# Identity products on TensorE at the start of two attention phases, an earlier load of the key bias, and a new order in cross-attention's first batch

## The chip, the core and the metric

The program runs on one core of a Trainium2 chip. The time is device microseconds from the start of the program to its end. A core has five engines with queues of their own: PE (TensorE, matrix products; its weight loads are a row of their own, PEld), DVE (VectorE), ACT (ScalarE), POOL (GpSimd) and SP (SyncE, which here issues all bulk DMAs). They meet only at semaphores, and each queue is worked off in program order. TensorE's clock has two levels in this trace, 1.2 and 2.4 GHz; the profile prints the granted clock as a share of the higher one, 0.50 or 1.00.

## What is computed

A post-norm decoder layer in float32: 16 batches of 100 tokens, width 512. Self-attention has 16 heads of 32, cross-attention 16 query heads and 4 key/value heads of 128 over a context of 361 tokens, and the last third is a mixture of 8 experts.

```python
x = _layernorm(x + _L0_attn_ref(x, w_q, w_k, w_v, w_o))
x = _layernorm(x + _L0_xattn_ref(x, ctx, mask, Wq, bq, Wk, bk, Wv, bv, Wo, qn_w, kn_w))
x = _layernorm(x + _L0_ffn_ref(x, ...))
...
# cross-attention
k = (encoder_hidden_states @ Wk + bk)   # 16 x 361 x 4 x 128
v = (encoder_hidden_states @ Wv + bv)
q, k = _rmsnorm(q, qn_w), _rmsnorm(k, kn_w)
probs = softmax(q k^T * scale + mask)
out = (probs v) @ Wo
```

## The kernel before

The program is a chain of blocks: self-attention over the batches, cross-attention over the batches, the experts. Between two blocks all engines meet at a barrier. Inside a block each engine has its own program, written out by hand in the order in which it is to be worked off, and `pe.wait_ge(sem, n)` makes the engine stand until another one has signalled. There is no scheduler: an instruction that waits holds back everything behind it on its engine.

Precision: the big products are done as three products of split operands. `product3` (L59 to L72; the product itself is L70) takes a high and a low part of each side and issues high by high, high by low and low by high. So each raw weight matrix is first split, the high part by ACT (`split_hi`) and the low part by DVE (`split_lo`), and TensorE waits for that (`w_lo`). Plain float32 products are used for the projections of q and k in self-attention (L258), the scores (L305), probabilities by values (L355) and all transposes (a product with the identity, `ident_s`).

Self-attention, first batch (`i == 0`). PE does the projections, the scores (L305), then waits for the split of w_v, does the value product on bank 7, transposes four groups of probabilities (L343) as POOL finishes each, multiplies them by the values (L355), projects the next pair's keys (L258), and does the output product on `a_woh`. From batch 1 on the queries of cross-attention (`a_Wqh`) are computed between those steps. After the last batch (`i == B`) three key products of cross-attention's first batch (`context_keys`) are laid between the last query work; the first of them waits for the context's low part (`head.ctx_lo`) and then for the split of Wk (`head.w_lo`, 2).

Cross-attention, before its loop. A batch's 361 context tokens are three chunks c of 121. Of each chunk there are keys (bias added, squared and summed on DVE in `key_squares`, the root on POOL, scaled on DVE in `key_norm`, transposed on PE in `transpose_keys`, split by ACT and DVE in `keys_hi` and `keys_lo`) and values (`values`, `values_hi`, `values_lo`). The bias bk is loaded by the first DMA of the block. DVE starts with `key_squares(0, 0)`, which needs it. PE does `values(0, c)` and `transpose_keys(0, c)` in turn for c = 0, 1, 2.

Cross-attention's loop. A batch j has four steps s, one for each key/value head, with four query heads h in each. PE interleaves the scores of step s, the transposes of the probabilities of the step before (`transpose_probs`, L855), parts of the keys of batch j + 1 and parts of the output product; `values_product` (probabilities by values of the step before) ends the step. In step 2 the order is: one quarter of the output product, `transpose_keys(j + 1, 0)`, the 12 products of `keys(j + 1, 2)`, and then `values_product`. Batch 0 has less work to interleave, since there is no batch before, and besides it ACT and DVE split the eight pieces of Wo, two at the end of each step.

## Time and profile before

| | us |
|---|---|
| median of 3 runs | 1596.74 |
| the runs | 1594.62 to 1597.72 |
| the profiled execution's own time | 1593.47 |
| its span | 1591.6 |
| PE busy | 1474.6 (93%) |
| DVE busy | 949.7 (60%) |
| mean granted clock of TensorE | 0.968 |

In rows of a timeline, the columns are the start in us, the duration in us (for a row that merges several instructions, from the start of the first to the end of the last), engine, source line, operation, tiles out<-in, partitions and shapes, and the count. In brackets stands the idle time of the engine right before it, and who ended it. Float32 products are recorded as two instructions each (x32 for 16 products). In rows of a table by windows, the columns are the stretch, its length, the busy time of each engine with instruction counts, the granted clock, the share of the DMA engines and GB/s.

### The profile page before, as it was taken

To read this page: it belongs to the slowest core of one execution; us is meant where nothing else is said; L and a number is where in the kernel's file an instruction comes from. 1 tells how busy PE (TensorE), PEld (TensorE's weight loads), DVE (VectorE), ACT (ScalarE), POOL (GpSimd) and SP (SyncE) were. 2 spreads that over 40 slices of the span, in tenths; PEclk is the share of its full clock that TensorE was granted. 3 is DMA by queue.
4 is the path that set the end of the run, shared out by engine and by line. 5 is a ranking of instruction groups with operands and counts; after the bars stand their busy time and mean duration, and the time that the engine had idled before them with its cause. 6 is when DMAs were issued, how large, how long until landed. Compare 5 with 4: busy or idle time off the path is not lost. (4 is left out here: it accounts for less than half of the span.)

```text
span 1591.6 us, 27704 instructions
## 1 busy us (share of the span) xinstructions
PE 1474.6 (93%) x8462; PEld 1206.2 (76%) x8462; DVE 949.7 (60%) x3585; ACT 662.4 (42%) x1789; POOL 648.4 (41%) x1000
## 2 busy tenths in 40 slices
PE   6999999999988689999999999999999999489967
PEld 6777877877866478888888888888888887367744
DVE  3666666666666565566655665566555665653457
ACT  4434334334343253444444444444444445343346
POOL 1324324324334364444444444344444443373164
PEclk8999999999999989999999999999999999789988
DMA  6221121121132332121111112111121213375373
GB/s 208 93 85 63 72 91 64 72 86 69 67 117 89 122 112 71 56 59 58 43 60 55 62 36 69 56 59 55 42 61 55 64 37 117 142 207 174 125 235 102
DMA packets 60669, 139.62 MB, mean 88 GB/s; under 512 B 10150, under 2 KB 20746, under 8 KB 59588
## 3 DMA queue, kind: packets, MB, share of 16 engines
q1 hardware_dynamic: 56008, 123.72, 23.5%
q0 software_dynamic: 4576, 14.95, 3.3%
q8 instruction: 31, 0.51, 0.1%
q14 instruction: 54, 0.44, 0.1%
HBM read 94.18 MB, written 44.46 MB: 87 GB/s over the span
## 5 line engine op out<-in xcount | busy, mean ns | idle before, releaser
L1253 POOL TENSOR_TENSOR b_pcarry<-b_half 128x1 f32<-128x1 f32 x173 | 47.6, 275 | 392.1 <-DVE b_rinv L1123 354.4
L1014 ACT ACTIVATE b_probs<-b_probs,b_nmax 100x361 f32<-100x361 f32 x256 | 152.1, 594 | 79.5 <-DVE b_nmax L1117 79.1
L70 PE MATMUL bank<-b_kTh,b_q 128*100 128x362 f32 x512 | 172.4, 337 | 9.3 <-DVE b_kTl L1099 6.0
L1117 DVE CUSTOM_DVE_ANT_0 b_probs<-bank,b_mask 100x361 f32<-100x361 f32 x256 | 135.3, 529 | 52.9 <-issue 45.2
L1278 POOL TENSOR_SCALAR b_probs<-b_probs,b_rinv 100x361 f32<-100x361 f32 x256 | 163.6, 651 | 0.0
L1110 DVE TENSOR_TENSOR b_pTl<-bank,b_pTh 121x400 fp32r<-121x400 f32 x192 | 109.7, 572 | 53.1 <-ACT b_pTh L1009 53.0
L1052 ACT ACTIVATE b_oTh<-bank,b_bv 128x400 fp32r<-128x400 f32 x64 | 38.1, 595 | 233.1 <-PE bank L70 233.1
L1009 ACT ACTIVATE b_pTh<-bank 121x400 fp32r<-121x400 f32 x192 | 96.6, 504 | 85.6 <-PE bank L855 81.3
L855 PE MATMUL bank<-ident,b_probs 100*121 100x100 f32 x768 | 111.3, 268 | 6.4 <-POOL b_probs L1278 5.6
L855 PEld LDWEIGHTS bank<-ident,b_probs 100*121 100x121 f32 x768 | 108.6, 188 | 9.0 <-POOL b_probs L1278 7.1
L70 PE MATMUL bank<-b_Woh,b_oTh 128*100 128x512 f32 x256 | 111.1, 434 | 1.4 <-DVE b_oTl L1181 1.4
L70 PEld LDWEIGHTS bank<-b_kTh,b_q 128*100 128x100 f32 x512 | 85.3, 167 | 29.3 <-issue 14.0
L70 PE MATMUL bank<-a_Wqh,a_x1Th 128*100 128x512 f32 x256 | 100.7, 393 | 2.7 <-DVE a_qn L547 1.5
L70 PE MATMUL bank<-a_Wqh,a_x1Tl 128*100 128x512 f32 x256 | 101.0, 394 | 0.0
L70 PE MATMUL bank<-b_Woh,b_oTl 128*100 128x512 f32 x256 | 100.9, 394 | 0.0
L70 PE MATMUL bank<-b_Wol,b_oTh 128*100 128x512 f32 x256 | 100.9, 394 | 0.0
L70 PE MATMUL bank<-a_Wql,a_x1Th 128*100 128x512 f32 x256 | 100.6, 393 | 0.0
L1181 DVE SCALAR_TENSOR_TENSOR b_oTl<-bank,b_bv,b_oTh 128x400 fp32r<-128x400 f32 x64 | 40.5, 633 | 97.6 <-ACT b_oTh L1052 97.6
L424 ACT ACTIVATE a_probs<-a_probs,a_nmax 100x100 f32<-100x100 f32 x256 | 92.8, 367 | 4.4 <-DVE a_nmax L500 4.4
L627 POOL TENSOR_TENSOR a_probs<-a_probs,a_rinv 100x400 f32<-100x400 f32 x64 | 54.7, 855 | 93.4 <-DVE a_rinv L507 93.3
L70 PE MATMUL bank<-b_Wkh,b_ctxh 128*121 128x512 f32 x192 | 82.2, 428 | 11.3 <-DVE b_kn L1080 8.2
L70 PE MATMUL bank<-b_kTl,b_q 128*100 128x362 f32 x256 | 84.3, 329 | 0.0
(259 smaller groups left out, 3949.4 us busy)
## 6 DMA issues: line engine op xcount, KB each, us to landing
b_q<-q_d SPq DMA_DIRECT2D x64, 400.0 KB, 3.1
q_d<-a_qo SPq DMA_DIRECT2D x62, 400.0 KB, 2.4
b_ctxr<-in_ctxT SPq DMA_DIRECT2D x48, 242.0 KB, 3.9
y_d<-c_y SPq DMA_DIRECT2D x32, 256.0 KB
c_Eraw<-in_expert_w SPq DMA_DIRECT2D x10, 512.0 KB, 7.0
a_stage<-in_Wq SPq DMA_DIRECT2D x4, 1024.0 KB
stage<-in_Wo SPq DMA_DIRECT2D x8, 512.0 KB, 4.4
a_xTr<-in_xT SPq DMA_DIRECT2D x8, 400.0 KB
```

The source lines that it names most:

```text
L70: mm = eng.matmul(out, lhsT=l(c), rhs=r(c), start=first and k == 0, stop=last and k == n - 1)
L424: e = act.activation(probs[:, r, c, :], probs[:, r, c, :], ACT.Exp, scale=-1.0, bias=nmax[:, h:h + 1], accum_out=psums[:, r, c:c + 1])
L627: pool.tensor_tensor(probs[:, r], probs[:, r], rinv[:, r].unsqueeze(2).to_broadcast([S, DC, S]), ALU.mult).then_inc(pn_rdy, 1)
L855: mm = pe.transpose(t_bank[c % 2][0:KT, h * S:(h + 1) * S], probs[:, s % 2, h, c * KT:(c + 1) * KT], ident_s[0:S, 0:S])
L1009: act.activation(pTh[:, c, :], t_bank[c % 2][0:KT, 0:XG * S], ACT.Copy).then_inc(pt_hi, 1)
L1014: act.activation(p, p, ACT.Exp, scale=-1.0, bias=nmax[:, s % 2, h:h + 1], accum_out=psums[:, s % 2, h:h + 1]).then_inc(e_rdy, 1)
L1052: act.activation(oTh[:, kv, :], o_bank[:, 0:XG * S], ACT.Identity, bias=bv_s[:, kv:kv + 1]).then_inc(o_hi, 1)
L1110: dve.tensor_tensor(pTl[:, c, :], t_bank[c % 2][0:KT, 0:XG * S], pTh[:, c, :].bitcast(F32), ALU.subtract).then_inc(pt_lo, 1)
L1117: dve.tensor_tensor_reduce(out=probs[:, s % 2, h, 0:SE], in0=s_bank[h % 2][0:S, 0:SE], in1=mask_s[:], scale=-1.0, scalar=BIG, op0=ALU.add, ...
L1181: dve.scalar_tensor_tensor(out=oTl[:, kv, :], in0=o_bank[:, 0:XG * S], scalar=bv_s[:, kv:kv + 1], in1=oTh[:, kv, :].bitcast(F32), op0=ALU.add,
L1253: pool.tensor_tensor(pcarry[:, k:k + 1], half_s[:, 0:1], half_s[:, 0:1], ALU.add)
L1278: pool.tensor_scalar(p, p, rinv[:, s % 2, h:h + 1], 1.0, ALU.mult, ALU.mult).then_inc(p_rdy, 1)
```

## The change

There are three parts.

1. `keep_busy(pe, out, ident, count)` issues `count` float32 products of the 128 x 128 identity with itself into a bank that is free at that place; nobody reads the result. It stands at seven places on PE: 8 before the wait for the split of w_v in self-attention's batch 0; 8, 4, 4 and 4 before the waits for the four groups of probabilities there; 12 between the two waits of `context_keys(0)`; 16 in cross-attention's batch 0 behind the first score of step 1, ahead of the first `transpose_probs`; 7 ahead of `transpose_keys(1, 1)`. That makes 63 products.
2. The load of bk is moved from the first DMA of cross-attention's block to SP's queue in batch `B - 2` of self-attention, into a tile that lives outside both blocks.
3. Cross-attention's first batch has another order: ahead of the loop on PE, ACT and DVE, and in step 2 of batch 0 on PE, where `values_product` now stands ahead of `keys(1, 2)`.

```diff
+def keep_busy(pe, out, ident, count):
+    for _ in range(count):
+        pe.matmul(out, lhsT=ident[:], rhs=ident[:], start=True, stop=True)
...
@@ self-attention, sync
                     for n in range(2):
                         sp.dma_start(head.pieces[n][1], head.pieces[n][0]).then_inc(head.w_raw[n], 16)
                         sp.dma_start(head.ctxr[:, n], ctxT[n]).then_inc(head.ctx_in[n], 16)
+                    sp.dma_start(head.bk_s[:], bk.partition_broadcast(KT)).then_inc(head.bk_in, 16)
@@ self-attention, tensor
                 pe.wait_ge(head.ctx_lo, c + 1)
+                if c == 0:
+                    keep_busy(pe, first_key_bank(bank, c)[:, 0:P], ident_s, 12)
                 pe.wait_ge(head.w_lo, 2)
...
                     if is_int and i == 0:
+                        keep_busy(pe, bank[6][:, 0:P], ident_s, 8)
                         pe.wait_ge(w_lo, 1)
...
                     for r in range(SR):
+                        if is_int and i == 0:
+                            keep_busy(pe, bank[6][:, 0:P], ident_s, 4 if r else 8)
                         pe.wait_ge(pn_rdy, 4 * i + r + 1)
@@ cross-attention, sync
-            sp.dma_start(bk_s[:], bk.partition_broadcast(KT)).then_inc(bk_in, 16)
             load_q(0, 0, 0)
@@ cross-attention, tensor
             def transpose_keys(jn, c):
-                pe.wait_ge(k_rdy, 3 * jn + c + 1)
                 if c == 1:
                     pe.wait_ge(kt_lo, 3 * jn + 1)
+                    if isinstance(jn, int) and jn == 1:
+                        keep_busy(pe, kv_bank[KEY_T_BANK[c]][:, 0:P], ident_s, 7)
+                pe.wait_ge(k_rdy, 3 * jn + c + 1)
...
-            for c in range(KC):
-                values(0, c)
-                transpose_keys(0, c)
+            values(0, 0)
+            values(0, 1)
+            transpose_keys(0, 0)
+            values(0, 2)
+            transpose_keys(0, 1)
+            transpose_keys(0, 2)
...
                         if now:
                             scores(j, s, h, par)
+                        if first and s == 1 and h == 0:
+                            keep_busy(pe, kv_bank[0][:, 0:P], ident_s, 16)
                         if before:
                             transpose_probs(n - 1, (s + 3) % 4, h)
...
                         if not last:
                             transpose_keys(j + 1, 0)
+                            if first:
+                                values_product(n - 1, s - 1, j)
                             keys(j + 1, 2)
...
-                    if before:
+                    if before and not (first and s == 2):
                         values_product(n - 1, (s + 3) % 4, j)
@@ cross-attention, vector, ahead of the loop
             key_squares(0, 1)
             key_norm(0, 0)
             values_lo(0, 0)
+            key_norm(0, 1)
+            key_squares(0, 2)
             keys_lo(0, 0, 0)
-            key_squares(0, 2)
-            key_norm(0, 1)
             values_lo(0, 1)
-            keys_lo(0, 1, 0)
             key_norm(0, 2)
             values_lo(0, 2)
+            keys_lo(0, 1, 0)
             keys_lo(0, 2, 0)
```

ACT's order ahead of the loop follows PE's: both value copies of chunks 0 and 1, then `keys_hi(0, 0)`, the value copy of chunk 2, then the other two `keys_hi`.

On DVE, ahead of cross-attention's loop, these rows stood behind the squares of chunk 1 before (`b_kn<-b_kn,b_krs` is `key_norm`, `b_Vl` is `values_lo`, `b_kTl` is `keys_lo`, `b_kn<-bank,b_bk` opens `key_squares` of chunk 2):

```order
L1093 TENSOR_TENSOR b_kn<-b_kn,b_krs 121x512
L1105 TENSOR_TENSOR b_Vl<-bank,b_Vh 121x512
L1099 TENSOR_TENSOR b_kTl<-bank,b_kTh 128x4x121
L1080 TENSOR_TENSOR b_kn<-bank,b_bk 121x512
...
L1093 TENSOR_TENSOR b_kn<-b_kn,b_krs 121x512
L1105 TENSOR_TENSOR b_Vl<-bank,b_Vh 121x512
L1099 TENSOR_TENSOR b_kTl<-bank,b_kTh 128x4x121
L1093 TENSOR_TENSOR b_kn<-b_kn,b_krs 121x512
L1105 TENSOR_TENSOR b_Vl<-bank,b_Vh 121x512
L1099 TENSOR_TENSOR b_kTl<-bank,b_kTh 128x4x121
```

and now, with the bias tile named bk:

```order
L1116 TENSOR_TENSOR b_kn<-b_kn,b_krs 121x512
L1128 TENSOR_TENSOR b_Vl<-bank,b_Vh 121x512
L1116 TENSOR_TENSOR b_kn<-b_kn,b_krs 121x512
L1103 TENSOR_TENSOR b_kn<-bank,bk 121x512
...
L1122 TENSOR_TENSOR b_kTl<-bank,b_kTh 128x4x121
L1128 TENSOR_TENSOR b_Vl<-bank,b_Vh 121x512
L1116 TENSOR_TENSOR b_kn<-b_kn,b_krs 121x512
L1128 TENSOR_TENSOR b_Vl<-bank,b_Vh 121x512
L1122 TENSOR_TENSOR b_kTl<-bank,b_kTh 128x4x121 x2
```

`key_norm` of chunk 1 has moved ahead of the squares of chunk 2, and the three `keys_lo` have moved behind the norms that TensorE's next transposes wait for.

On PE, step 2 of cross-attention's batch 0, the end of the step stood like this before (`b_kn` is `transpose_keys(1, 0)`, `b_Wkh` the keys of chunk 2, `b_pTh` is `values_product`, `b_kTh` the next step's score):

```order
L893 MATMUL bank<-ident,b_kn 128x121 x4
L70 MATMUL bank<-b_Wkh,b_ctxh 121x512
L70 MATMUL bank<-b_Wkl,b_ctxh 121x512
L70 MATMUL bank<-b_Wkh,b_ctxl 121x512
...
L70 MATMUL bank<-b_pTh,b_Vh 128x400
L70 MATMUL bank<-b_pTl,b_Vh 128x400
L70 MATMUL bank<-b_pTh,b_Vl 128x400
...
L70 MATMUL bank<-b_kTh,b_q 100x362
```

and now:

```order
L906 MATMUL bank<-ident,b_kn 128x121 x4
L70 MATMUL bank<-b_pTh,b_Vh 128x400
L70 MATMUL bank<-b_pTl,b_Vh 128x400
L70 MATMUL bank<-b_pTh,b_Vl 128x400
...
L70 MATMUL bank<-b_Wkh,b_ctxh 121x512
L70 MATMUL bank<-b_Wkl,b_ctxh 121x512
L70 MATMUL bank<-b_Wkh,b_ctxl 121x512
...
L70 MATMUL bank<-b_kTh,b_q 100x362
```

The nine products of `values_product` have changed places with the twelve of the keys.

## Rows read from the trace of the kernel before

**Rows 1.** The page, busy time of each engine.
```profile
PE 1474.6 (93%) x8462; PEld 1206.2 (76%) x8462; DVE 949.7 (60%) x3585; ACT 662.4 (42%) x1789; POOL 648.4 (41%) x1000
```

**Rows 2.** Table by windows, one stretch near each phase's start.
```profile
26.00:27.00 1.00, 1.00 (x3) 0.59 (x3) 1.00 (x1) 0.00 (x0) 0.00 (x0) 0.50 0.64 98
...
600.00:605.00 5.00, 5.00 (x24) 4.21 (x23) 1.92 (x9) 1.83 (x5) 0.00 (x0) 0.72 0.56 201
```

**Rows 3.** PE's timeline, self-attention's first batch, and one step of the second.
```profile
14.69 5.58 PE L258 MATMUL bank<-a_xTr,a_wq 128*128 128x200 f32 x32
...
25.07 0.45 PE L70 MATMUL bank<-a_wvh,a_xTh 128*100 128x512 f32 x1 [1.94 <-DVE a_wvl L463]
...
34.99 0.91 PE L343 MATMUL bank<-ident,a_probs 100*100 100x100 f32 x4 [0.54 <-POOL a_probs L627]
35.82 3.56 PE L355 MATMUL bank<-a_pT,a_v 100*32 100x100 f32 x32
39.31 7.48 PE L258 MATMUL bank<-a_xTr,a_wk 128*128 128x200 f32 x32
46.49 0.53 PE L70 MATMUL bank<-a_woh,a_oTh 128*100 128x512 f32 x1
...
49.16 0.39 PE L70 MATMUL bank<-a_woh,a_oTl 128*100 128x512 f32 x1
...
70.64 1.99 PE L355 MATMUL bank<-a_pT,a_v 100*32 100x100 f32 x32
```

**Rows 4.** PE's timeline, the first key product behind self-attention's last batch.
```profile
503.58 0.57 PE L70 MATMUL bank<-b_Wkh,b_ctxh 128*121 128x512 f32 x1 [3.10 <-DVE b_Wkl L468]
...
506.50 0.63 PE L70 MATMUL bank<-b_Wkl,b_ctxh 128*121 128x512 f32 x1
```

**Rows 5.** DVE's timeline, cross-attention ahead of its loop.
```profile
532.11 0.07 DVE L1128 MEMSET b_probs<- 100x16 f32 x1
536.33 0.69 DVE L1080 TENSOR_TENSOR b_kn<-bank,b_bk 121x512 f32<-121x512 f32 x1 [4.14 <-DMA b_bk<-in_bk]
...
539.59 0.68 DVE L1093 TENSOR_TENSOR b_kn<-b_kn,b_krs 121x512 f32<-121x512 f32 x1
```

**Rows 6.** POOL's timeline, the root of the second chunk's sums.
```profile
540.41 1.01 POOL L1269 TENSOR_TENSOR b_krs<-b_krs,b_half 121x4 f32<-121x4 f32 x1
```

**Rows 7.** PE's timeline, cross-attention ahead of its loop and the first score.
```profile
532.14 0.46 PE L70 MATMUL bank<-b_Wvh,b_ctxh 128*121 128x512 f32 x1 [2.10 <-PEq L105]
...
540.33 1.07 PE L893 MATMUL bank<-ident,b_kn 121*128 121x121 f32 x4 [5.15 <-DVE b_kn L1093]
...
551.05 0.38 PE L70 MATMUL bank<-b_kTh,b_q 128*100 128x362 f32 x1 [1.65 <-DVE b_kTl L1099]
```

**Rows 8.** PE's timeline, batch 0, from step 1 to the first transposes of step 2.
```profile
559.13 1.13 PE L855 MATMUL bank<-ident,b_probs 100*121 100x100 f32 x4 [4.41 <-POOL b_probs L1278]
...
564.33 0.63 PE L70 MATMUL bank<-b_Wkh,b_ctxh 128*121 128x512 f32 x1
...
570.00 0.67 PE L855 MATMUL bank<-ident,b_probs 100*121 100x100 f32 x4
```

**Rows 9.** DVE's timeline, batch 0: masked scores, first and last of step 2, first of step 3.
```profile
571.75 0.53 DVE L1117 CUSTOM_DVE_ANT_0 b_probs<-bank,b_mask 100x361 f32<-100x361 f32 x1
...
575.15 0.53 DVE L1117 CUSTOM_DVE_ANT_0 b_probs<-bank,b_mask 100x361 f32<-100x361 f32 x1
...
588.77 0.53 DVE L1117 CUSTOM_DVE_ANT_0 b_probs<-bank,b_mask 100x361 f32<-100x361 f32 x1
```

**Rows 10.** PE's timeline, batch 0, end of step 2 to end of step 3.
```profile
576.41 0.63 PE L893 MATMUL bank<-ident,b_kn 121*128 121x121 f32 x4
580.50 0.76 PE L70 MATMUL bank<-b_Wkh,b_ctxh 128*121 128x512 f32 x1 [3.46 <-DVE b_kn L1080]
...
585.74 0.35 PE L70 MATMUL bank<-b_pTh,b_Vh 121*128 121x400 f32 x1
...
598.12 0.63 PE L893 MATMUL bank<-ident,b_kn 121*128 121x121 f32 x4 [1.88 <-DVE b_kn L1093]
```

More of the change, by code:

```diff
@@ L96, in first_key_bank, with self_attention_phase @@
     return bank[(0, 1, 7)[c]]
-def self_attention_phase(nc, sem, head, ctxT, x_nat, xT, w_q, w_k, w_v, w_o, Wq, bq, qn_w, kn_w, causal, ident, ident_s, x1_d, q_d):
+def self_attention_phase(nc, sem, head, ctxT, bk, x_nat, xT, w_q, w_k, w_v, w_o, Wq, bq, qn_w, kn_w, causal, ident, ident_s, x1_d, q_d):
     with ExitStack() as ctx:
@@ L676, in cross_attention_phase @@
         mask_s = sb("b_mask", [S, SE])
-        bk_s = sb("b_bk", [KT, XKV * XHD])
+        bk_s = head.bk_s
         bv_s = sb("b_bv", [P, XKV])
@@ L1026, in expert_hi @@
                 act.activation(first_pieces[n][2], first_pieces[n][1], ACT.Copy).then_inc(e_hi, 1)
-            for c in range(KC):
-                values_hi(0, c)
-                keys_hi(0, c, 0)
+            values_hi(0, 0)
+            values_hi(0, 1)
+            keys_hi(0, 0, 0)
+            values_hi(0, 2)
+            keys_hi(0, 1, 0)
+            keys_hi(0, 2, 0)
             act.wait_ge(consts, 32)
```

17 lines of the change are left out of this document (9 added, 8 removed).

## The prediction

> **What bounds the kernel.** I read the page first: TensorE is busy for 93% of the span [rows 1], so the loops are bound by it and only places where it stands still or runs at the low clock can give time back. Then the table by windows, for the granted clock: it is 1.00 through nearly all of both loops and 0.50 in a few stretches at the phases' starts [rows 2]. Then PE's timeline there. In self-attention's first batch PE waits 1.94 us for the split of w_v and again before each group of transposes, and what follows runs at 1.2 GHz: the product on `a_pT` takes 3.56 us where the same 16 products in batch 1 take 1.99 [rows 3]. At cross-attention's start PE waits 5.15 us, since DVE waited 4.14 us for the DMA of bk [rows 5, 7]. In batch 0 there are waits of 4.41, 3.46 and 1.88 us [rows 8, 10]. Behind these places PE is nearly always busy, so time gained there should reach the end.
>
> **What an identity product costs.** The trace has none. The nearest row is the projection of q: 16 products, 200 columns wide, in 5.58 us at the high clock, 0.349 each [rows 3]. By columns (128/200) one costs 0.223 us, which I take; 0.349 is the upper bound at this clock, if width does not matter, and twice 0.223, 0.446, is the price at the low clock. The lower bound is nothing beyond the wait it stands in. 63 of them are 14.0 us of work laid into waits; where they outlast the wait, the rest is paid.
>
> A rule of the Trainium skill (TensorE: Matmul & The Clock Gate, LDWEIGHTS) has a weight load take the number of columns over 1.2 ns: 107 ns for 128. With two loads per float32 product, as the x32 for 16 suggests, that gives at least 0.21 us if the streaming is hidden beside it, and some 0.43 if not; by the second figure the groups of four would each outlast their wait.
>
> **Start of self-attention.** The first 8 (1.8 us) fit in the 1.94 us wait, and the clock should not fall. The next 8 stand behind the value product, which ends about 1.7 us earlier at the high clock (12 products at 0.243 instead of about 0.42), and end before the first probabilities. The groups of 4 cost 0.9 us; the waits for POOL are 0.5 to 1.0 us beside transposes at the low clock, which shorten too, so I cost them at nothing; at 0.349 each they would be 0.4 us late three times. The transposes themselves follow ACT and POOL, and do not move. Behind them: the last transposes end 0.4 us earlier, the product on `a_pT` goes from 3.56 to 1.99 (1.57), the projection from 7.18 us (39.31 to 46.49, low clock for its first half) to about 5.7 (the 5.58 of the other one and its tail), 1.5. Sum 3.4 us. The other inputs are there: the split behind the output product is done on DVE at about 41 us, and the new projection ends at 43. Bounds: 0 if the clock falls again, 4 if all of it holds. Low side: minus 2 (below).
>
> **End of self-attention.** PE waits 3.10 us for the split of Wk and then runs at the low clock, from 503.58 to 506.50 seven spacings of 0.417 [rows 4]; at the high clock a product of this width is spaced (49.16 - 46.49)/11 = 0.243 [rows 3]. The 12 identity products (2.7 us) fit in the wait. About eight key products run low, 8 x 0.18 = 1.4 us; behind them waits the transposition of x1, whose input DVE has ready before PE takes it, by its timeline. Gain 1.2 us, bounds -1 (12 x 0.349 = 4.2) and 1.4.
>
> **Cross-attention ahead of the loop.** The load of bk has moved about 90 us earlier, where SP issues it in a third of a microsecond among loads that nothing waits for soon; I cost it at nothing, since PE is fed from loads of the batches before. `load_q(0, 0, 0)` moves up by one issue. DVE then starts at 532.2 instead of 536.33: 4.1 us [rows 5]. From there I follow both queues. The first norm stands 3.26 us behind the start [rows 5]: 535.5, done 536.1. PE does two value groups, 532.14 to 537.8 (24 x 0.24 = 5.7), and the transposes of chunk 0 to 538.2, without the wait of 5.15 us [rows 7]. The norm of chunk 1 follows at 537.3: the second sums are ready at 535.5, and POOL takes 1.8 us with its root of 1.01 [rows 6]. The squares of chunk 2 wait for the transposes and stand at 538.35 to 540.0, the norm of chunk 2 at 542.0, its transposes on PE at 542.7, ACT's copy at 543.3, and the last `keys_lo` at 543.85 to 544.5. The first score starts at 544.6 instead of 551.05 [rows 7]: 6.4 us. Of these 4.1 are the load and 2.3 the order and the clock, which no longer falls. DVE is the last in this chain, not PE. Bounds: 4.1 if only the load counts, 7 if the queues pack tighter.
>
> **Batch 0, step 1.** Behind the first score of step 1, PE waits 4.41 us for POOL [rows 8]. 16 x 0.223 = 3.6 us fit. The stretch 559.13 to 564.33 then lasted 5.2 us at the low clock without a wait; at the high clock PE needs half of it and DVE becomes the bound: in step 2 it needs 3.4 us from the first to the last masked score (571.75 to 575.15) [rows 9]. Gain 5.2 - 3.4 = 1.8 us. The transposes of step 2 at 570.00 follow POOL, which follows the last exponential, so the gain arrives there; bounds 0.5 and 2.6.
>
> **Step 2.** After the transposes at 576.41 PE waits 3.46 us for the bias addition of chunk 1's keys, which DVE reaches behind the splits of Wo [rows 9, 10]. `values_product` does not need it: 9 products of 400 columns, 0.243 x 400/512 x 9 = 1.7 us, now lie in this wait. The keys begin at the same place after the wait, 580.4, and if the clock holds they take 2.8 us instead of 5.24 (580.50 to 585.74): 2.4. Together 4.1 us on PE, of which DVE lets some 3.2 to 4 through: it masks step 3's first score behind the squares of chunk 2, by 585.6 instead of 588.77 [rows 9].
>
> **Step 3.** The wait before the transposes of chunk 2 at 598.12 [rows 10] ends with DVE's norm, which stands 5.3 us behind the last masked score; that moves by the 4 us. The 7 products (1.6 us) stand ahead of it: PE is there at 591.7 on the old scale, done at 593.2, and the norm is due at 594.1. Costed at nothing; 0.9 us is the margin, which at 0.349 each would be just used up. Steps 2 and 3 together: 4.0 us, bounds 1 and 5.5 (the short low-clock stretch behind 600 us could go as well [rows 2]).
>
> **Sum.** 3.4 + 1.2 + 6.4 + 1.8 + 4.0 = 16.8 us. Against the profiled execution, 1593.47, this gives 1576.7; the median of the runs lies 3.3 us above it, and I carry that over: 1596.74 - 16.8 = 1579.9, rounded to 1580. Nothing in the experts' part is touched. Its own low-clock stretches could come out a little different, since all of it starts earlier; I take 2 us either way for that.
>
> **Rivals.**
> A. The clock falls in self-attention's first batch all the same. For it: between the groups of four stand transposes and short waits, and PE fell to 0.50 there with the engine partly busy. Then the groups cost 4 x 0.446 = 1.8 us where about 1.0 is free, 0.8 late three times, the term of 3.4 turns into about -2: 1580 + 5 = 1585.
> A sentence of the Trainium skill (same page, Part 4: PE-mode transpose) speaks for it: transposes do not count as busy for the clock in the way other products do. By it only the identity products would hold the clock there.
> B. DVE and the Wo splits are the bound in batch 0. For it: DVE ends the waits at 551.05, 580.50 and 598.12 [rows 7, 10]. Against it: after the splits it stands idle itself, and the Wo pieces land before ACT asks for them. Then the 1.8 and 4.0 shrink to about 1 in all: 1585.
> C. More than the sum: the fall at 600 us goes as well and DVE's chain packs tighter: 1575.
> D. Slower. The identity products do not hold the clock, and each costs 0.446. Then they outlast their waits: 63 x 0.446 = 28.1 us against some 15.1 us of waits (1.9 + 1.0 + 2.7 + 3.1 + 4.5 + 1.9), 13 us late. Against that stand only the load of bk and the order, 4.1 + 1.7 + 0.5: net 6.6 us slower, 1603. It turns at a cost of (15.1 + 6.3)/63 = 0.34 us each, if no clock is gained. Against it: float32 projections keep the clock at 1.00 while they run.
> E. No change: what starts earlier waits later, at the barrier or in the loop. Against it: in the loops PE's waits are few and short. 1597.
>
> **Chances.** The sum 60%, A 14%, B 10%, C 10%, D 4%, E 2%. The range that holds 8 in 10 is 1574 to 1588: the sum with its bounds, C, and A and B with some of each together. Within 0.2% (3.2 us), about what the measurement can tell from no change: 0.02; slower 0.04; faster 0.94.
>
> **What would show it.** The granted clock at 1.00 from 25 to 50 us, around 504, 538 to 545 and 558 to 565 us. The identity products at 0.22 us each; a wait behind each group of them, not in front of it: if the transposes of probabilities start later than before, the groups are too long. `a_woh` 3.4 us earlier. In cross-attention the bias addition at the memsets, the first score 12.4 us after the start of the block's first product instead of 18.9, the transposes of step 1 8.1 us behind it as before, and from the block's first product to the transposes that stood at 598.12 some 12 us less than the 66.0 of before. The prediction is wrong if these distances hold and the end does not move, or if the clock still reads 0.50 behind an identity group.

## The result and the profile after

The changed kernel takes 1573.61 us (median of 4 runs, 1573.55 to 1574.31), the kernel before in the same comparison 1595.68 (4 runs, 1591.64 to 1597.72): ratio 0.988, 95% interval 0.9863 to 0.9897. That is 22 us less by the medians and 19 by the ratio, where the sum said 16.8. A second comparison on another chip gave 1573.58 against 1590.26 (6 and 11 runs), ratio 0.9898 [0.9877, 0.9918], 16 to 17 us less. The kernel before is the one that wanders: single runs lie between 1586.4 and 1597.7, and its medians in the three comparisons below are 1592.13, 1591.38 and 1590.26 (53 runs), some 5 us under the 1596.74 from which the prediction started.

The page of the changed kernel, busy time and granted clock (PEclk, the span in 40 slices, in tenths of full speed): as many microseconds on TensorE as before [rows 1], 126 instructions more, in a span of 1571.8 us instead of 1591.6.

```profile
span 1571.8 us, 27953 instructions
PE 1474.6 (94%) x8588; PEld 1208.8 (77%) x8588; DVE 949.9 (60%) x3585; ACT 662.0 (42%) x1789; POOL 646.4 (41%) x1000
PEclk9999999999999999999999999999999999689988
```

That the busy time is the same with 63 products more is the first thing to see: what they add, the rest saves by running at 2.4 GHz.

PE's timeline, self-attention's first batch (columns: start, us, engine, line, operation, tiles, count, and the wait before it with what ended it), to set beside [rows 3]:

```profile
22.24 2.05 PE L78 MATMUL bank<-ident 128*128 128x128 f32 x16
24.16 0.47 PE L70 MATMUL bank<-a_wvh,a_xTh 128*100 128x512 f32 x1
...
26.98 1.95 PE L78 MATMUL bank<-ident 128*128 128x128 f32 x16
30.73 0.55 PE L355 MATMUL bank<-ident,a_probs 100*100 100x100 f32 x4 [1.79 <-POOL a_probs L639]
31.11 1.08 PE L78 MATMUL bank<-ident 128*128 128x128 f32 x8
32.17 0.55 PE L355 MATMUL bank<-ident,a_probs 100*100 100x100 f32 x4
...
35.54 2.00 PE L367 MATMUL bank<-a_pT,a_v 100*32 100x100 f32 x32
37.46 5.68 PE L265 MATMUL bank<-a_xTr,a_wk 128*128 128x200 f32 x32
42.84 0.53 PE L70 MATMUL bank<-a_woh,a_oTh 128*100 128x512 f32 x1
```

An identity product costs (24.16 - 22.24)/8 = 0.24 us. The transposes of probabilities still follow each other by 1.44 us, with the groups of four in place of the waits. The product on `a_pT` takes 2.00 us instead of 3.56, and `a_woh` starts 3.65 us earlier, of which 0.82 was there already at the scores, ahead of all identity products (20.09 us after, 20.91 before).

The same view at cross-attention's first keys, at its first score, and in batch 0, to set beside [rows 4, 7, 8, 10]:

```profile
492.59 2.84 PE L78 MATMUL bank<-ident 128*128 128x128 f32 x24
495.94 0.50 PE L70 MATMUL bank<-b_Wkh,b_ctxh 128*121 128x512 f32 x1 [0.51 <-DVE b_Wkl L480]
...
533.65 0.63 PE L906 MATMUL bank<-ident,b_kn 121*128 121x121 f32 x4 [0.75 <-DVE b_kn L1116]
535.73 0.59 PE L70 MATMUL bank<-b_kTh,b_q 128*100 128x362 f32 x1 [1.45 <-DVE b_kTl L1122]
...
540.21 3.73 PE L78 MATMUL bank<-ident 128*128 128x128 f32 x32
544.92 0.67 PE L866 MATMUL bank<-ident,b_probs 100*121 100x100 f32 x4 [0.98 <-POOL b_probs L1301]
...
554.14 0.67 PE L866 MATMUL bank<-ident,b_probs 100*121 100x100 f32 x4 [1.22 <-POOL b_probs L1301]
...
564.65 0.47 PE L70 MATMUL bank<-b_Wkh,b_ctxh 128*121 128x512 f32 x1 [1.81 <-DVE b_kn L1103]
...
567.99 0.57 PE L866 MATMUL bank<-ident,b_probs 100*121 100x100 f32 x4
```

The first score is 15.3 us earlier than in [rows 7]; the wait of 5.15 us has shrunk to 0.75. But the score's product takes 0.59 us where [rows 7] has 0.38: PE had run at the high clock, stood still for 0.75 and 1.45 us, and now the low clock falls on the scores.

DVE's timeline at the same place, to set beside [rows 5]: no wait for `bk`.

```profile
523.42 0.07 DVE L1151 MEMSET b_probs<- 100x16 f32 x1
523.48 0.69 DVE L1103 TENSOR_TENSOR b_kn<-bank,bk 121x512 f32<-121x512 f32 x1
```

The table by windows (columns: window, length, busy time and count of PE, its loads, DVE, ACT and POOL, then the clock):

```profile
26.00:27.00 1.00, 1.00 (x7) 0.70 (x6) 1.00 (x1) 0.00 (x0) 0.00 (x0) 1.00 0.94 392
24.50:42.00 17.50, 15.71 (x127) 14.05 (x126) 9.21 (x44) 12.40 (x41) 3.41 (x4) 1.00 0.42 142
502.00:506.00 4.00, 4.00 (x19) 2.83 (x18) 1.90 (x10) 0.25 (x1) 0.20 (x1) 1.00 0.00 0
523.50:526.90 3.40, 3.40 (x15) 2.69 (x16) 3.22 (x19) 0.38 (x1) 1.21 (x2) 1.00 0.76 185
535.90:539.30 3.40, 3.40 (x12) 2.79 (x12) 1.45 (x8) 1.38 (x4) 0.00 (x0) 0.52 0.00 0
544.00:552.00 8.00, 7.08 (x41) 6.34 (x42) 5.17 (x19) 5.71 (x13) 7.24 (x13) 1.00 0.72 215
564.60:568.00 3.40, 3.35 (x16) 2.77 (x17) 1.25 (x9) 0.00 (x0) 1.49 (x3) 1.00 0.73 272
```

Of these only the stretch of the first scores is near 0.5.

Cut into stretches by starts on PE's timeline (us), the profiled executions compare like this. "Start" is from self-attention's first scores to batch 0's `x1` transposes; "last but one" from batch 13's `x1` transposes to batch 14's; "last" from there to the first product on `Wkh`; "Wk keys" from that to the first product on `Wvh` of cross-attention's block; "to score" from there to the first score; "to step 1" from that to the first transposes of probabilities in step 1; "step 1" and "step 2" from there to those of steps 2 and 3. The rows below the fourth are the experiments of the next section, in their order.

| kernel | start | last but one | last | Wk keys | to score | to step 1 | step 1 | step 2 |
|---|---|---|---|---|---|---|---|---|
| before | 31.93 | 28.69 | 28.21 | 28.56 | 18.91 | 8.08 | 10.87 | 17.87 |
| before, again | 31.28 | 28.82 | 27.70 | 28.56 | 18.84 | 8.08 | 10.87 | 15.47 |
| changed | 29.09 | 26.72 | 26.23 | 27.51 | 12.28 | 9.19 | 9.22 | 13.85 |
| changed, again | 28.95 | 26.70 | 26.61 | 27.52 | 12.27 | 9.21 | 9.21 | 13.84 |
| identity alone | 28.24 | 26.72 | 26.47 | 27.56 | 18.73 | 8.07 | 9.23 | 17.04 |
| load alone | 31.72 | 28.97 | 27.62 | 28.35 | 13.88 | 8.83 | 10.88 | 18.03 |
| load and order | 30.06 | 28.63 | 28.87 | 27.47 | 13.82 | 8.97 | 10.87 | 15.41 |
| identity at start | 28.23 | 26.72 | 27.54 | 28.31 | 18.79 | 8.09 | 10.87 | 17.02 |
| narrow at start | 32.65 | 26.73 | 26.11 | 28.57 | 18.87 | 8.08 | 10.87 | 17.82 |
| no step 1 | 28.28 | 26.71 | 26.99 | 27.05 | 13.83 | 9.15 | 10.87 | 15.40 |
| no groups of 4 | 31.36 | 26.72 | 26.03 | 27.55 | 13.81 | 9.20 | 9.22 | 13.82 |
| old step 2 | 28.21 | 26.69 | 27.85 | 27.52 | 12.28 | 8.97 | 9.22 | 18.24 |
| more places | 28.20 | 26.70 | 27.03 | 27.16 | 13.80 | 8.08 | 9.22 | 13.83 |
| 20 more at start | 31.02 | 26.80 | 27.55 | 27.54 | 12.25 | 8.96 | 9.23 | 13.85 |

From batch 0 to 13 every kernel takes 393.8 to 394.1 us. Before and changed differ by 19.0 us in these stretches and by 0.8 ahead of the first scores, where nothing was edited; what follows step 2 adds 0. The second pair, before again and changed again, differs by 15.3 us in the same stretches (15.2 in the span). Most of the distance between the two pairs lies in step 2, 4.0 against 1.6 us.

The length of "last" goes with the clock in it. In the five kernels whose mean granted clock there is 1.00 it takes 26.0 to 26.6 us; in seven at 0.93 or 0.94, 27.0 to 27.9; in before at 0.92, 28.2; in load and order at 0.84, 28.9.

### The profile page after: what moved, and what is told of

Read it like the earlier page. It is cut to its first block and busy times, and to the rows that moved or that the text cites. A ratio compares the mean times of both kernels' runs of the same rounds, so it can differ in the third digit from the quotient of the medians.

```text
span 1571.8 us, 27953 instructions
## 1 busy us (share of the span) xinstructions
PE 1474.6 (94%) x8588; PEld 1208.8 (77%) x8588; DVE 949.9 (60%) x3585; ACT 662.0 (42%) x1789; POOL 646.4 (41%) x1000
## 5 line engine op out<-in xcount | busy, mean ns | idle before, releaser
L70 PEld LDWEIGHTS bank<-b_kTh,b_q 128*100 128x100 f32 x512 | 85.1, 166 | 28.9 <-issue 13.9
```

The costliest lines, as they stand in the source:

```text
L70: mm = eng.matmul(out, lhsT=l(c), rhs=r(c), start=first and k == 0, stop=last and k == n - 1)
```

## The experiments

**The kernel before, again** (nothing changed): how far does it wander?

> The kernel before, unchanged, run against itself. In the profiled execution of before, one store of queries took 4.8 us to land instead of 2.5, TensorE waited 2.97 us in self-attention's last batch and its clock fell from 473 to 480 us; together some 4 us that the change does not explain. Theory T (an accident of that execution): the ratio is 1.000, single runs lie from 1591 to 1598 as those so far, and the new profile shows no such wait, but perhaps another. Theory U (it belongs to the kernel's schedule): the same wait and the same fall at 473 us are there again.

Ratio 0.9998 [0.9984, 1.0012], 1590.95 us (1586.58 to 1596.04, 12 runs). Its profiled execution has a span 5.7 us shorter than the first one's (1585.9): 1.6 ahead of the first scores, 2.4 in step 2, 0.65 at the start, 0.5 in the last batch. In step 2 both wait 3.46 us ahead of the keys; behind it the clock is 0.50 from 578.9 to 585.7 us in the first execution, and 1.00 through the whole step in the repeat. So in one and the same program the clock falls in one execution and not in another. Theory U was right, though: the wait ahead of batch 14's `x1` transposes is there again, 3.12 us, and the fall of the clock at 473 us behind it.

**The identity products alone**, with load and order as before:

```diff
+                    if is_int and i == 0:
+                        keep_busy(pe, bank[6][:, 0:P], ident_s, 8)
 ...
+                        if first and s == 1 and h == 0:
+                            keep_busy(pe, kv_bank[0][:, 0:P], ident_s, 16)
```

> The 63 identity products at their seven places, with the order and the bk load of before. By the sum of terms: start of self-attention 3.4 to 3.7 us, its end 1.1, step 1 of batch 0 1.7, step 3 0 to 1; the waits of 5.15 and 3.46 us stay and with them the clock's falls behind them. So 6 to 8 us faster than before, ratio about 0.9955. Rival (the identity products also steady the loops, since runs of before differ by 6 us and runs of the changed kernel by 0.8): 10 to 12 us faster, ratio 0.993, and a narrow spread.

Ratio 0.9941 [0.9917, 0.9964], 9.4 us (11.7 by the medians). The start takes 28.24 us, step 1 9.23, the keys 27.56. And a stretch that the prediction had not named is shorter: the last but one, 26.72 us instead of 28.7.

**The load of bk alone:**

```diff
+                    sp.dma_start(head.bk_s[:], bk.partition_broadcast(KT)).then_inc(head.bk_in, 16)
 ...
-            sp.dma_start(bk_s[:], bk.partition_broadcast(KT)).then_inc(bk_in, 16)
```

> Only the load of bk is moved; order as before, no identity products. By the sum: DVE's wait of 4.1 us goes, and the first score comes 4.1 us earlier; ratio 0.9974. Rival (PE or another queue takes the wait's place, for instance the values' high parts on ACT): 0 to 2 us. Second rival (with the shorter wait the clock does not fall any more): up to 6 us.

Ratio 0.9974 [0.9963, 0.9985], 4.1 us. The way to the first score shrinks by 5.0 us (18.9 to 13.88), and the scores behind it lose 0.75 of these to the low clock.

**Load and order without identity products:**

```diff
-            pe.matmul(out, lhsT=ident[:], rhs=ident[:], start=True, stop=True)
```

> The changed kernel with all counts of identity products at zero: the load and the new order alone. By the sum: 4.1 us for the load, 2.3 for the order ahead of the loop, 1.7 for values_product in the wait of step 2 and up to 2.4 if the clock then holds there; 8 to 10 us faster than before, ratio 0.994 to 0.995. Rival (the order is worth nothing without the identity products, because the clock falls anyway): 4 to 5 us, ratio 0.997.

Ratio 0.9956 [0.994, 0.9972], 7.0 us. With the 9.4 of the identity products that makes 16.4 us for the parts, and the whole gave 16.2 (0.0102 of 1590.3) and 19.1 (0.012 of 1595.7): with intervals of 2 to 4 us either way they add up.

The way to the first score, 13.82 us, looks like that of the load alone, 13.88, but the clock differs. With the load alone it is 1.00 all the way; here it is low from 530.4 to 533.8 us, on the values products. Where the clock falls there in kernels with this order the way takes 13.8 us (here, without step 1's products, without the groups of 4, with more places), and where it doesn't, 12.3 (changed, its repeat, old step 2, 20 more at start). The first values products in the kernel without step 1's products, to set beside 523.50:526.90 of the changed kernel in the table above:

```profile
523.80:527.20 3.40, 3.40 (x8) 2.62 (x9) 3.22 (x19) 0.00 (x0) 1.21 (x2) 0.50 0.77 193
```

So at the same clock the new order is worth 1.6 us (13.88 to 12.3).

**Identity products at self-attention's start alone** (28 on the kernel before):

```diff
+                        keep_busy(pe, bank[6][:, 0:P], ident_s, 8)
 ...
+                            keep_busy(pe, bank[6][:, 0:P], ident_s, 4 if r else 8)
```

> The kernel before with the 28 identity products of self-attention's first batch alone. In the kernels without them (before, its repetition, load alone, no identity products) one store of queries at 463 to 470 us lands after 4.8 to 5.1 us, and TensorE waits 2.9 to 3.3 us in the last batch; in the two with them it lands after 2.8 at most and the wait is 1.0. Theory P (place of the program: 56 more instructions in PE's queue shift the point at which PE's next block of instructions is fetched away from these stores): 3.0 to 3.7 us at the start, and 2 to 4 more at 470 us; 1586 us, ratio 0.9965 to 0.9955. Rival T (the stretch at 470 us depended on something else of the change): 3.5 us in all, ratio 0.998.

Ratio 0.9965 [0.9953, 0.9978], 5.6 us. Against the repeat of before, the trace has 3.1 at the start and 2.1 in the last but one batch, 400 us behind the last identity product, where nothing was edited.

**The same 28, eight columns wide:**

```diff
-        pe.matmul(out, lhsT=ident[:], rhs=ident[:], start=True, stop=True)
+        pe.matmul(out[:, 0:8], lhsT=ident[:], rhs=ident[:, 0:8], start=True, stop=True)
```

> As e5, with the 28 products made 8 columns wide instead of 128: as many instructions, little streaming. Theory P: the clock falls at the start as in the kernel before (no gain there), but the store at about 465 us lands in under 3 us and TensorE's wait in the last batch is 1 us: 2 to 4 us faster, ratio 0.998. Rival (it was the earlier time and not the number of instructions): the store takes 4.8 us again, ratio 1.000.

Ratio 0.998 [0.9969, 0.9991], 3.2 us. PE's timeline, and the table by windows behind its first identity products:

```profile
22.50 1.95 PE L78 MATMUL bank<-ident 128*128 128x8 f32 x16
24.43 0.47 PE L70 MATMUL bank<-a_wvh,a_xTh 128*100 128x512 f32 x1
...
33.65 0.89 PE L352 MATMUL bank<-ident,a_probs 100*100 100x100 f32 x4
...
36.76 3.56 PE L364 MATMUL bank<-a_pT,a_v 100*32 100x100 f32 x32
```

```profile
24.50:42.00 17.50, 17.50 (x105) 15.60 (x106) 8.51 (x43) 11.59 (x40) 3.41 (x4) 0.62 0.33 121
```

Eight narrow products take as long as eight wide ones (1.93 and 1.92 us from start to the next product). PE is busy for all of the 17.5 microseconds, with no wait left between the transposes, and its clock falls twice nonetheless, from 25.3 to 28.8 and from 32.2 to 42.4 us: mean 0.62, as in the kernel before (0.64, busy for 13.6 of 17.5). The changed kernel is busy for less, 15.7 us, and holds 1.00. The start is 0.7 to 1.4 us longer than in the kernel before, since at the low clock a group of four takes 1.55 to 1.62 us and delays the transposes behind it. But the last but one batch takes 26.73 us here too. So that gain is not the clock's; it comes with the number of PE's instructions.

**The changed kernel without the 16 of step 1:**

```diff
-                        if first and s == 1 and h == 0:
-                            keep_busy(pe, kv_bank[0][:, 0:P], ident_s, 16)
```

> The changed kernel without the 16 identity products in step 1 of cross-attention's batch 0. By the sum the clock falls in the wait of 4.4 us, and step 1 runs at 1.2 GHz: 1.8 us slower than the changed kernel, 1575.4. Rival (the fall costs only what TensorE does not wait for anyway): 0.5 us or less. Second rival (the clock then stays low into step 2): 3 to 4 us.

Ratio 0.9912 [0.9891, 0.9933], which the interval does not set apart from the changed kernel's 0.9898. In the trace the wait and the low clock of before are back, and step 1 takes 10.87 us, 1.65 more. Step 2 takes 15.40 us, 1.55 more: the clock falls again behind the 1.83 us wait ahead of the keys, where the changed kernel waits 1.81 us and keeps 1.00 (564.60:568.00 above). PE's timeline at both waits, and the clock behind the second:

```profile
546.73 1.13 PE L866 MATMUL bank<-ident,b_probs 100*121 100x100 f32 x4 [4.51 <-POOL b_probs L1299]
...
568.10 0.70 PE L70 MATMUL bank<-b_Wkh,b_ctxh 128*121 128x512 f32 x1 [1.83 <-DVE b_kn L1101]
```

```profile
568.10:571.50 3.40, 3.40 (x8) 2.65 (x9) 1.02 (x8) 0.00 (x0) 1.45 (x3) 0.51 0.73 267
```

Load and order, the other kernel with the new order and without the 16, has 15.41 us in step 2; the five traces with both (changed, its repeat, no groups of 4, more places, 20 more at start) have 13.82 to 13.85. So in the traces the 16 go with 3.2 us, about what the second rival had. Why a fall of the clock in step 1 should be followed by one in step 2 isn't shown.

**The changed kernel without the three groups of 4** (their count 0, the 8 ahead of them stay):

```diff
-                            keep_busy(pe, bank[6][:, 0:P], ident_s, 4 if r else 8)
+                            keep_busy(pe, bank[6][:, 0:P], ident_s, 0 if r else 8)
```

> The changed kernel without the three groups of 4 between the transposes of the first batch's probabilities; the two groups of 8 stay. If the clock needs them: it falls between 30 and 36 us, the product on a_pT takes 3.5 us and the projection 7.4, 3 to 3.5 us slower than the changed kernel, 1577. Rival (they fill a wait that cost nothing): within 0.5 us of it.

Ratio 0.9899 [0.9883, 0.9916], which by itself can't be told from the changed kernel's; the trace can tell. The transposes wait again, the clock is at 0.50 from 33.5 to 40.4 us, and the start takes 31.36 us, as in the kernels without identity products there (30.1 to 31.9):

```profile
29.15 0.55 PE L355 MATMUL bank<-ident,a_probs 100*100 100x100 f32 x4 [0.85 <-POOL a_probs L639]
...
33.48 0.90 PE L355 MATMUL bank<-ident,a_probs 100*100 100x100 f32 x4 [0.90 <-POOL a_probs L639]
34.31 3.56 PE L367 MATMUL bank<-a_pT,a_v 100*32 100x100 f32 x32
```

All of the start's gain hangs on the 12 products between the transposes. The two groups of 8 hold the clock over the value product (1.00 from 25 to 29 us, 0.62 before) and shorten nothing by that, since the transposes follow POOL.

That transposes do not hold the clock as other products do (the Trainium skill, TensorE: Matmul & The Clock Gate, Part 4) agrees with this trace. The waits of 0.9 us between them would explain this kernel as well, but not the one with narrow products, where the clock falls without such waits.

**The changed kernel with the values product of step 2 at its old place:**

```diff
-                            if first:
-                                values_product(n - 1, s - 1, j)
                             keys(j + 1, 2)
 ...
-                    if before and not (first and s == 2):
+                    if before:
```

> The changed kernel with one of its moves undone: in cross-attention's step 2 of the first batch the products of probabilities and values stand again behind the next batch's last keys, where the kernel before has them; the identity products, the earlier load and the rest stay. The sum of the prediction: in the kernel before step 2 took 17.9 us from its first transposes of probabilities to those of step 3 (and 15.5 in a repeat of it), with a wait for the output projection's split weights and a fall of the clock behind it; in the changed kernel it took 13.9. If the move is what shortens it, this kernel takes 1 to 2 us more than the changed one there and the whole time is 0.06 to 0.13% longer. The rival: the repeat shows that most of the 4 us came and went with the clock (15.4 us also in the variant without the 16 identity products of step 1), so the move itself is worth nothing: the stretch stays at 13.9 us and the time within 0.5 us.

Ratio 0.991 [0.9891, 0.9929]; 1577.18 us against 1573.58 in the same comparison. By the ratios the two can't be told apart; the trace can tell more. Step 2 takes 18.24 us, 4.4 more, of which 0.7 comes back in step 3. The rows of PE and the clock behind the wait, in this kernel:

```profile
565.45 0.75 PE L70 MATMUL bank<-b_Wkh,b_ctxh 128*121 128x512 f32 x1 [3.46 <-DVE b_kn L1101]
```

```profile
564.70:571.50 6.80, 6.05 (x15) 4.80 (x16) 2.12 (x11) 0.00 (x0) 2.20 (x4) 0.50 0.43 149
```

Without the nine products in it the wait is 3.46 us again, as in [rows 10] (1.81 in the changed kernel), and the clock falls behind it. The rival, that step 2 stays at 13.9 us, is out. How much the move is worth depends on the clock: over seven traces with the old place step 2 takes 15.5 to 18.2 us, 17.4 on average, and over five with the new place and the 16 products 13.8. At the clock of 1.00 it is 1.6 us (15.47 in the repeat of before, 13.85), which is the wait's 1.65; the rest, up to 2.8, is a fall that the new place had in none of the five.

**Identity products in four more waits** of the changed kernel:

```diff
+            keep_busy(pe, kv_bank[0][:, 0:P], ident_s, 3)
             transpose_keys(0, 2)
+            keep_busy(pe, y_bank[:, 0:P], ident_s, 6)
 ...
+            keep_busy(pe, h_bank[0][:, 0:P], ident_s, 14)
             transpose_slots(0)
 ...
+            keep_busy(pe, t_bank[0][:, 0:P], ident_s, 40)
             pe.wait_ge(pb_split, 3)
```

> The changed kernel with identity products in four more waits: 3 ahead of the last transposes of cross-attention's first keys and 6 ahead of the first scores (waits of 0.75 and 1.45 us there), 14 ahead of the experts' first transposes (wait of 5.4 us) and 40 in the wait ahead of the combining stage (10.9 us). If a fall of the clock behind a wait is the cost, the first scores run at the high clock (1.1 us less until the transposes of step 1: 9.2 us in the changed kernel, 8.1 where the clock held), the expert products right behind the wait take 0.40 us and not 0.63 each (about 2.5 us less), and the combining stage's transposes and first products likewise (about 1.2 us less): up to 4.8 us, about 1569 us. The rival: TensorE already stands at the low clock when the 14 products ahead of the experts begin, each takes near 0.45 us, and they outlast the wait or end with it, so that the experts gain nothing; the whole is then 1 to 2 us faster, or not at all.

Ratio 0.9904 [0.9883, 0.9926], 1575.46 us (1570.99 to 1580.16) against 1573.58: no gain. The clock is held and the end does not follow. PE at the experts' start:

```profile
1373.13 5.17 PE L78 MATMUL bank<-ident 128*128 128x128 f32 x28
1378.59 0.66 PE L1547 MATMUL bank<-ident,c_xg 128*128 128x128 f32 x4 [0.28 <-DMA c_xg<-x_d,c_tok]
...
1381.08 0.39 PE L1570 MATMUL bank<-Esplit,c_xgl 128*128 x1
```

The 14 run at 0.37 us each, partly at the low clock, and just fit; the first expert products take 0.39 us each instead of 0.63. Counted from the products on `c_Z`, the last of them ends 1.3 us earlier than in the first trace of the changed kernel, and the program 0.8 earlier; but in the second trace of the changed kernel, without these products, both come 0.4 and 0.9 us earlier still. So no gain is shown there. At the first scores 0.4 us is lost: they do run at the high clock (8.08 us to step 1), but start 1.5 us later, since the clock is low on the values products (523.6 to 527.0 us), ahead of the first of the added ones. That low stretch is in two kernels without them too (no step 1, no groups of 4).

**Twenty more identity products at the start** of the changed kernel (8 ahead of the first transposes become 28):

```diff
-                            keep_busy(pe, bank[6][:, 0:P], ident_s, 4 if r else 8)
+                            keep_busy(pe, bank[6][:, 0:P], ident_s, 4 if r else 28)
```

> The changed kernel with 20 more identity products ahead of self-attention's first transposes of probabilities, where a wait of 1.8 us covers 8 of them. It asks what made the stretch between the x1 transposes of the last two batches of self-attention 2 to 3 us shorter in the changed kernel (26.7 us, before 28.5). The theory: TensorE fetches its instructions by a transfer of its own, and what counts is where this falls among the four stores of q. In the kernel before it is at 467.5 us, among the stores, one of which lands after 4.8 us; in the changed kernel at 471.1 us, behind them, and the slowest lands after 2.8 us. 12 identity products more moved it 3.4 us earlier against the batch, so 20 more bring it back among the stores (about 465.5 us with the batch as in the changed kernel): one store lands after 4.5 to 5 us, TensorE waits about 3 us ahead of the x1 transposes, the stretch takes 28.5 us again, and the kernel is 4 to 6 us slower than the changed one (2.9 from the products that outlast their wait, 2 to 3 from the store). The rival: the short store comes from TensorE's own state or from a transfer of another engine; the stores still land within 2.9 us, the stretch takes 26.7 us, and the kernel is 2.9 us slower and no more.

Ratio 0.9934 [0.9917, 0.9951], 1579.86 us, 6.3 more than the changed kernel beside it; by the traces it is 3.6 us late at the first `Wkh` product and 5.4 at the end. The slowest store's time to landing, and the wait ahead of the `x1` transposes:

```profile
DMA to landing us min/median/max: 2.4/2.5/2.9
```

```profile
472.10 0.93 PE L331 MATMUL bank<-ident,a_x 100*128 100x100 f32 x4 [1.10 <-DVE a_x L610]
```

The fetch did come among the stores, 3.15 us after the first one's issue, as that pair of stores ended, and nothing was late: the stretch took 26.80 us. That is what the rival said. But earlier in the same kernel, in the stores from 72.5 us on, a fetch began 3.28 us after the first store, and the second landed after 4.8 us, where every other kernel has 2.8. What this leaves of the theory is weighed below.

**The changed kernel again:**

> The changed kernel once more, beside its three variants on the same chip. The first measurement had 4 runs of it; the profiled one has a gain of 20 us, 3 to 4 of which stand behind the one late store of the second-to-last batch of self-attention. If the ratio of 0.988 holds, it takes about 1573 to 1577 us here; if its first runs were lucky, as a repeat of the kernel before varied by 9 us from run to run, the ratio comes out nearer to 0.991.

Ratio 0.9898 [0.9877, 0.9918], 1573.58 us (1570.49 to 1577.65).

## Where the two microseconds of the last but one batch come from

In this batch the `x1` transposes wait for DVE, which waits for ACT's buffer `a_qo`, which waits for the store of q. The transposes in the changed kernel, against 2.97 us of waiting at the same place of the kernel before:

```profile
469.71 0.56 PE L331 MATMUL bank<-ident,a_x 100*128 100x100 f32 x4 [1.01 <-DVE a_x L610]
```

The stores' times to landing there, in the kernel before and in the changed one:

```profile
DMA to landing us min/median/max: 2.3/2.5/4.8
```

```profile
DMA to landing us min/median/max: 2.3/2.4/2.8
```

And the DMA queues while the first store runs (columns: packets, MB, share of the 16 engines), in the kernel before from 466.2 to 468.4 us, in the changed one from 462.7 to 464.8:

```profile
q1 hardware_dynamic: 274, 0.78, 89.3%
q8 instruction: 1, 0.02, 3.8%
```

```profile
q1 hardware_dynamic: 260, 0.73, 87.3%
```

The packet of q8 is a fetch of instructions, 16,384 bytes in one piece on one DMA engine for 1.3 us, where the store's pieces are 3,200 bytes. A batch of self-attention has four stores of q, in two pairs. In the 14 traces together that makes 224 groups of four, and 19 of them have a store that takes over 4 us (4.1 to 5.1), called slow below:

- In 197 groups no fetch begins within 6 us of the first store. None of them has a store above 3.2 us.
- In 16 a fetch begins 2.1 to 2.9 us after the first store. The second is slow in all 16.
- In 10 it begins 3.1 to 3.5 us after it. The second is slow in two, load and order at 463 us and 20 more products at 72.5 us.
- In one it begins 5.7 us after it, during the second pair, and the fourth store is slow (no groups of 4, at 490 us).

The slow stores move with the number of identity products ahead of them: with none they are at about 103 and 464 us, with 16 at 102 and 490, with 28 at about 130 alone, with 48 at 72.5 alone. 28 products make the fetch come some 10 us earlier against the batch, narrow ones as well as wide ones. At the last but one batch the four kernels without identity products at the start have the slow store, and these four have the stretch of 28.6 to 29.0 us, the other ten 26.7 to 26.8.

What sets the two slow ones of the ten apart from the other eight can be read from the packets: whether some of the second store's are still to come when the fetch begins. The DMA queues from the fetch's start, in load and order (466.27 to 467.6 us, slow) and with 20 more products (467.06 to 468.5, not slow):

```profile
q8 instruction: 1, 0.02, 4.4%
q1 hardware_dynamic: 2, 0.01, 3.1%
```

```profile
q8 instruction: 1, 0.02, 5.4%
q1 hardware_dynamic: 1, 0.00, 0.0%
```

In the first, two packets of 3,200 bytes are left; they begin when the fetch's 0.94 us are over. In the second none is left (the one packet has 4 bytes). The same holds for all 19 slow stores and for the eight that aren't: packets left in the 19, none in the eight.

The slow store also costs time behind itself: TensorE's wait of 2.9 to 3.3 us is followed by a low clock, which is part of what "last" takes in those four kernels.

Shown is that the gain of 2 us comes with the number of instructions ahead of it and not with the clock (the narrow products), and that a store is slow where a fetch falls into the end of its pair, and nowhere else. The experiment brought the fetch just behind the last packet at one place, and made a new slow store at another. Why so small a transfer delays a store by 2 us isn't shown; packets left are not enough for it, since the first store of the pair, which in 15 of these cases had packets left too, still lands after 2.4 to 2.9 us.

The Trainium skill (Runtime: NRT & Kernel Launch, Instruction fetch mechanics) has each engine's sequencer fetch blocks of 16 KiB, 256 instructions, by a DMA queue of its own; the packet's size agrees. It calls the cost of crossing into a new block mostly hidden. Here TensorE does not wait for the fetch itself in this stretch, but the store beside it costs 2 us.

## Why the prediction was right, and where its sizes were off

The mechanism was right: identity products in waits hold the clock, and the earlier load and the new order shorten the way to the first score. The measured terms of the profiled pair add up to 16.2 us for the 16.8 of the sum.

- **Price of a product.** 0.223 us forecast. Measured from start to next product, 0.22 (28 in a row), 0.23 (16), 0.24 (8) and 0.23 to 0.27 (4) at the high clock. All groups fitted their waits. Width played no part below 128 columns. That agrees with the rule on weight loads of the Trainium skill (TensorE: Matmul & The Clock Gate, LDWEIGHTS) as the prediction quotes it, 0.21 us with the streaming hidden. Its 0.43 for streaming that isn't hidden is too high for this clock: a product of 512 columns is spaced 0.23 us, so two passes of 128 columns would bring some 0.12 on top of 0.21, by estimate 0.33.
- **Start, 3.4 us.** 2.8 in the profiled pair; over all traces the stretch takes 28.2 to 29.1 us with the groups as in the changed kernel and 30.1 to 31.9 without. Rival A needed the groups to fail; the kernel without them shows its clock, the changed one does not.
- **End of self-attention, 1.2 us.** The keys take 1.05 us less, and the wait for the split fell from 3.10 to 0.51 us. But load and order, without any identity product, has 27.47 us for the keys too: there the clock had fallen ahead of the wait (496.3 to 499.7 us) and was back at 1.00 behind it. No kernel leaves out the 12 products alone, so their own share isn't shown.
- **Ahead of the loop, 6.4 us.** 6.63 measured: the load 5.0 (4.1 forecast), the order 1.6. The clock's fall was said to be gone. It has moved onto the first scores and costs 1.1 us there; in the kernels without step 1's products, without the groups of 4 and with more places it falls on the values products as well or instead, which costs 1.5. The step that failed is the sentence that the clock "no longer falls": the waits of 0.75 and 1.45 us were not in the sum. For this reason the transposes of step 1 come 9.2 us behind the first score and not 8.1 as foretold.
- **Step 1, 1.8 us.** 1.65, in the pair and by the kernel without the 16. That the 16 also keep a fall of the clock out of step 2, 1.55 us, was not in the term.
- **Steps 2 and 3, 4.0 us.** 4.0 to the transposes of step 3 in the profiled pair. Of these 1.6 are the shorter wait and 2.4 a fall of the clock that the profiled execution of before had and its repeat had not; by the averages over all traces it is 3.5. So that the term came out to the tenth is luck. To the same transposes of batch 1 there are 0.45 more (64.97 to 64.52 us), since the fall at 600 us is gone; the loops behind lose them again. What the 7 products brought isn't shown: load and order, without them, takes as long in the step behind.
- **What the sum lacked.** The last but one batch, 2.0 us; the last one, 2.0, which goes with the clock in it (0.92 to 1.00); a loss of 1.1 at the scores; and 0.8 ahead of the first scores, a time that differs by up to 1.8 us between traces. 16.2 + 4.0 - 1.1 + 0.8 = 19.9 us in the profiled pair. From the start of cross-attention's block to the transposes that stood at 598.12, the distance foretold as 12 us shorter is 10.5 shorter.
- **The base.** The median of three runs, 1596.74, was carried over. The 53 later ones have medians of 1590 to 1592, so the base was about 5 us too high, and with it the forecast of 1580 for a measured 1573.6. Against the later runs the changed kernel gains 16 to 17 us on the same chip, which is the sum's size; but it is so with 2 us of it in a batch that no term named, and with falls of the clock that come and go. That closeness is in part luck.
- **Rivals.** B, E and D are out: DVE does end the waits left in batch 0 (1.81 us at 564.65), but step 1 gave what was forecast and the end moved. C is the closest by its time, 1575. Its fall at 600 us did go, but brought nothing at the end, and DVE's chain packed hardly tighter than the sum had it (6.6 for 6.4).

## What to carry to other kernels

A wait of one to four microseconds on TensorE costs twice where the clock falls behind it. Products on an identity, 128 columns wide here, counted to end just before the wait does, take the second half back, but only where TensorE is also what the next microseconds wait for. Count the waits that are left after the edit: the fall can go to the next uncovered one, as it went to the first scores here. Compare two traces stretch by stretch with the clock beside each, since a fall that came by lot looks like an effect of the edit. Before a gain is credited to an edit, look for stretches that were shortened far from it, and take the base from as many runs as the difference asks for.

## What the runs showed of the hardware that was not expected

- TensorE busy for 17.5 microseconds out of 17.5 at a mean granted clock of 0.62 (24.5 to 42.0 us with narrow products), and for 15.7 out of 17.5 at 1.00 with wide ones at the same places. The busy time in the profile does not say which level is granted.
- Where an instruction fetch of 16,384 bytes began while packets of the last store in flight were still to come, that store landed after 4.1 to 5.1 us, in 19 cases of 19. With a fetch just behind the last packet (eight cases) and without any (197) none took over 3.5 us.
- A float32 product of 128 by 128 weights takes 0.24 us at the high clock whether 8 or 128 columns stream, in groups of eight.
- The same program's runs differ by up to 10 us (1586.4 to 1596.0 in one comparison). Between its two traces, 2.4 of 5.7 us are one fall of the clock, in step 2.
